# A graph network on one core: self terms moved into an eighth bank between Q and P, thirds and squares given to GpSimd, unread products put ahead of two stages

## What is computed

```python
h = relu(layernorm(x)); x = x + L0(h)                    # two hyperbolic passes inside L0
h = relu(layernorm(x))
src = [edge_src, all nodes]; dst = [edge_dst, all nodes] # a self edge for every node
m = relu(concat(h[src], h[dst]) @ W1 + b1)               # 128 wide
out = segment_sum(m @ W2 + b2, dst) / counts             # counts include the self edge
x = x + out
```

## Time and profile before

| | |
|---|---|
| median of 3 runs | 1189.39 us (1187.72 to 1190.02) |
| the profiled execution: own time, and its span | 1186.87 us, 1185.0 us |
| busy: PE, PEld, DVE, ACT, POOL | 1028.0, 951.0, 1054.7, 712.7, 368.7 us |
| seam 1, from the first fold to the first product of the second pass | 488.75 to 527.21 us |
| seam 2, from the first sum to the spread of group 1 | 636.44 to 700.26 us |
| the edge loop from there | 484.7 us |

### The profile page before, as it was taken

The page is one execution under the profiler, slowest core; times in us unless marked ns, Lnnn a source line. Parts: engine busy times, 40 slices in busy tenths (PEclk is TensorE's granted clock), DMA queues, the critical chain, the costliest instruction groups (busy, mean ns, idle before and its releaser), DMA issues.

```text
span 1185.0 us, 53692 instructions
## 1 busy us (share of the span) xinstructions
PE 1028.0 (87%) x21722; PEld 951.0 (80%) x21722; DVE 1054.7 (89%) x1448; ACT 712.7 (60%) x1933; POOL 368.7 (31%) x268
## 2 busy tenths in 40 slices
PE   3079898989898998728998599999999999999998
PEld 2058777777787877727998479999999999999997
DVE  8879999999999999785664889999999999999995
ACT  5348888888888888520002576665556555666663
POOL 7000000000000000010000037777777777777774
PEclk9569999999999999759999689999999999999999
DMA  2002323232323232579950255444544445444450
GB/s 82 0 33 100 122 95 126 95 126 95 126 95 126 95 122 99 228 284 337 411 244 18 86 172 164 162 160 152 157 156 159 158 159 161 161 161 161 161 161 29
DMA packets 44877, 169.98 MB, mean 143 GB/s; under 512 B 19440, under 2 KB 19766, under 8 KB 44827
## 3 DMA queue, kind: packets, MB, share of 16 engines
q1 hardware_dynamic: 44827, 169.28, 39.7%
HBM read 121.11 MB, written 48.14 MB: 143 GB/s over the span
## 4 chain that ended last, share of the span: by engine, by line
PE 51%; DVE 32%; issue 9%; DVEq 4%; ACT 2%; DMA 1%; SPq 0%; POOL 0%; ACTq 0%; POOLq 0%
PE PS L1563 17%; PE PS L1565 11%; PE PS L1578 8%; PE PS L1436 8%; DVE arena L1055 7%; DVE arena L1032 5%; DVE arena L1040 4%; DVE arena L1018 3%; PE PS L1583 3%; DVE arena L1027 2%; DVEq L361 2%; PE PS L1467 1%; DMA Cw<-slot_rows 1%; DVE arena L1047 1%; DVE aggTw L1066 1%
## 5 line engine op out<-in xcount | busy, mean ns | idle before, releaser
L595 POOL TENSOR_TENSOR arena<-arena 128x512 bf16<-128x512 f32 x240 | 342.3, 1443 | 319.6 <-ACT arena L773 319.6
L1563 PE MATMUL PS<-arena 125*128 125x128 bf16 x3600 | 344.6, 219 | 2.5 <-DVE HTw L1268 1.0
L773 ACT ACTIVATE arena<-arena 128x512 bf16<-128x512 f32 x240 | 150.8, 628 | 187.1 <-DVE arena L1285 187.1
L1563 PEld LDWEIGHTS PS<-arena 125*128 125x128 bf16 x3600 | 250.4, 97 | 9.3 <-issue 5.1
L1436 PE MATMUL PS<-arena,A 125*64 125x72 f32 x4800 | 179.3, 230 | 65.0 <-DVE aggTw L1066 38.4
L1436 PEld LDWEIGHTS PS<-arena,A 125*64 125x64 f32 x4800 | 165.4, 139 | 74.3 <-issue 49.5
L653 ACT ACTIVATE arena<-arena 128x72 bf16<-128x72 bf16 x864 | 216.9, 344 | 1.7 <-DVE arena L1040 1.7
L1285 DVE SCALAR_TENSOR_TENSOR arena<-PS,arena 128x512 f32<-128x512 f32 x240 | 159.4, 679 | 28.7 <-ACT arena L780 28.7
L780 ACT ACTIVATE arena<-PS 128x512 bf16<-128x512 f32 (+2 forms) x336 | 171.9, 547 | 0.0
L1565 PE MATMUL PS<-arena 108*128 108x128 bf16 x1200 | 167.4, 221 | 0.0
L1565 PE MATMUL PS<-arena,HTw 108*128 108x128 bf16 x1200 | 165.8, 219 | 0.0
(11 more groups left out here) (195 smaller groups left out, 1388.5 us busy)
## 6 DMA issues: line engine op xcount, KB each, us to landing
adjacency<-arena SPq DMA_DIRECT2D x48, 900.0 KB, 3.6
arena<-adjacency SPq DMA_DIRECT2D x46, 900.0 KB, 8.0
Bw<-slot_rows SPq DMA_DIRECT2D x48, 800.0 KB, 4.2
Cw<-slot_rows SPq DMA_DIRECT2D x48, 700.0 KB, 4.5
arena<-q_table SPq DMA_DIRECT2D x144, 18.0 KB
q_table<-arena SPq DMA_DIRECT2D x6, 336.0 KB
slot_rows<-slot_row SPq DMA_DIRECT2D x49, 13.0 KB
x_sb<-in_x SPq DMA_DIRECT2D x1, 700.0 KB
```

The source lines that it names most:

```text
L595: nc.gpsimd.tensor_tensor(H3[k][:, at_b, 2, :], Hs[k][:, 4 * q:4 * q + 4, :], H3[k][:, at_b, 1, :], ALU.subtract).then_inc(s_low_set, 1)
L773: nc.scalar.activation(H3[k][:, at_b, 1, :], Hs[k][:, 4 * q:4 * q + 4, :], ACT.Copy).then_inc(s_mid_set, 1)
L1563: mm(ps, OTs[k][:, b, :], P3[:, b, part, :], start=(part == 0), stop=False)
```

## The change

What it does, by place in the program:

- **Self terms** (`self_sum_ps(c)` is the first columns of bank 7): PE makes each quad's self term in bank 7, one bank for all seven, between the Q products: Q0, Q1, S0, Q2, S1, ... Q6, S5, P0, S6, P1 to P6. Each waits until the relu of the one before has emptied the bank (`self_set`). DVE takes the relu instead of ACT, in the iteration of its Q loop that is two quads later.
- **Thirds**: all thirds of Q, and those of the first `PLOWS` = 3 quads of P, are GpSimd's. `spread(0)` waits for the thirds of P quad by quad instead of for all.
- **Squares of seam 1**: GpSimd makes the first `POOLED` = 4, DVE the last 3. The two memsets become eight of at most `CLEAR` = 800 columns, `aggTw` first, before `rows_ps` is waited for.
- **Unread products**: `keep_warm` issues 50 bf16 products of 128x128 by 128 columns, whose result is not read, before the second pass (released by `due` in the middle of `linear(1)`) and before the transposes (released by `due` behind the first sums of the layer norm).
- The first load to `Cw` is released when the layer norm's squares are summed (`squares_summed`). The addition of the bias b2 moves behind the one-hot matrices of group 0's sums.

```diff
@@ -40,6 +40,10 @@
 OWN = 4096.0
+PLOWS = 3
+WARM = 50
+POOLED = 4
+CLEAR = 800
 WHOLE = 12582912.0
...
@@ -459,7 +470,7 @@
                 load_sources(0)
-                sp.wait_ge(norm_in, 2 * len(PIECES))
+                sp.wait_ge(squares_summed, 1)
                 load_destinations(0)
...
@@ -575,12 +586,19 @@
                 if l == 1:
+                    for c in range(POOLED):
+                        pool.wait_ge(fold_set, c + 1)
+                        pool.tensor_tensor(quad_of(square_words, c), quad_of(aggTw[0:F, :], c),
+                                           quad_of(aggTw[0:F, :], c), ALU.mult).then_inc(sq_first, 1)
                     with pool.If(fast == 1):
                         pool.wait_ge(ht_set, len(QUADS))
-                        pool.wait_ge(sq_set, len(QUADS))
-                        pool.wait_ge(rows_ps, 1)
-                        pool.memset(degree, 0.0).then_inc(agg_cleared, 1)
-                        pool.memset(aggTw[:, :], 0.0).then_inc(agg_cleared, 1)
+                        pool.wait_ge(sq_first, POOLED)
+                        pool.wait_ge(sq_rest, len(QUADS) - POOLED)
+                        for table in (aggTw, degree):
+                            if table is degree:
+                                pool.wait_ge(rows_ps, 1)
+                            for a in range(0, NW, CLEAR):
+                                pool.memset(table[:, a:min(a + CLEAR, NW)], 0.0).then_inc(agg_cleared, 1)
                 with pool.If(fast == 0):
...
@@ -600,7 +618,18 @@
+            def quad(table, c):
+                return table[:, QUADS[c][0]:QUADS[c][-1] + 1]
             with pool.If(fast == 1):
+                for c in range(len(QUADS)):
+                    pool.wait_ge(q_second, c + 1)
+                    pool.tensor_tensor(quad(Q3, c)[:, :, 2, :], quad(RQ, c), quad(Q3, c)[:, :, 1, :],
+                                       ALU.subtract).then_inc(q3_set, 1)
+                for c in range(PLOWS):
+                    pool.wait_ge(p_second, c + 1)
+                    pool.tensor_tensor(quad(P3, c)[:, :, 2, :], quad(RP, c), quad(P3, c)[:, :, 1, :],
+                                       ALU.subtract).then_inc(p3_first, 1)
                 turns(pool, low_parts)
...
@@ -761,12 +790,6 @@
-            for c, bs in enumerate(QUADS):
-                sc.wait_ge(self_ps, c + 1)
-                nc.scalar.activation(RT[:, 0:N].rearrange("f (p b) -> f b p", b=NB)[:, bs[0]:bs[-1] + 1, :],
-                                     bank(c)[:, 0:PN * len(bs)].rearrange("f (b p) -> f b p", p=PN),
-                                     ACT.Relu).then_inc(self_set, 1)
             def middle(g, k, q):
...
@@ -854,10 +876,12 @@
-            def layer_norm(dst, source):
+            def layer_norm(dst, source, second=False):
...
                     link(ve.tensor_reduce(row(T1)[:, b], source[:, b, :], X, ALU.add))
+                if second:
+                    ve.sem_inc(due, 1)
                 for b in PIECES:
...
@@ -865,6 +889,8 @@
                     link(ve.tensor_reduce(row(T2)[:, b], C[:, b, :], X, ALU.add))
+                if second:
+                    ve.sem_inc(squares_summed, 1)
                 ask(ve.tensor_scalar(a_, row(T2), 1.0 / F, 1e-5, ALU.mult, ALU.add))
...
@@ -919,6 +945,8 @@
                 ts(row(ATN), row(T3), ARTANH[0], ALU.mult)
+                if l == 1:
+                    ve.sem_inc(due, 1)
                 for c in ARTANH[1:]:
...
@@ -1197,10 +1225,10 @@
                                          quad_of(aggTw[F:2 * F, :], c), ALU.add).then_inc(fold_set, 1)
-                    for c in range(len(QUADS)):
+                    for c in range(POOLED, len(QUADS)):
                         ve.wait_ge(fold_set, c + 1)
                         ve.tensor_tensor(quad_of(square_words, c), quad_of(aggTw[0:F, :], c),
-                                         quad_of(aggTw[0:F, :], c), ALU.mult).then_inc(sq_set, 1)
+                                         quad_of(aggTw[0:F, :], c), ALU.mult).then_inc(sq_rest, 1)
                     ve.wait_ge(rows_ps, 1)
...
@@ -1245,17 +1273,26 @@
             tt(x_sb[:, :, :], x_sb[:, :, :], A[:, :, :], ALU.add)
-            layer_norm(A[:, :, :], x_sb[:, :, :])
+            layer_norm(A[:, :, :], x_sb[:, :, :], True)
...
             ts(row(Z), row(Z), 1.0, ALU.add, 1.0, ALU.max)
+            ve.sem_inc(counts_read, 1)
             link(ve.reciprocal(row(Z), row(Z)))
-            tt(x_sb[:, :, :], x_sb[:, :, :], b2b[P_, :].unsqueeze(1).broadcast_to([PN, NB, F]), ALU.add)
             link(ve.memset(RT[:, N:NW], 0.0))
...
                 return table[:, QUADS[c][0]:QUADS[c][-1] + 1]
+            def add_bias():
+                ve.tensor_tensor(x_sb[:, :, :], x_sb[:, :, :], b2b[P_, :].unsqueeze(1).broadcast_to([PN, NB, F]),
+                                 ALU.add).then_inc(bias_set, 1)
+            def self_relu(c):
+                ve.wait_ge(self_ps, c + 1)
+                ve.tensor_scalar(quad_of(RT, c), self_sum_ps(c).rearrange("f (b p) -> f b p", p=PN), 0.0, None,
+                                 ALU.max).then_inc(self_set, 1)
...
@@ -1295,21 +1332,25 @@
                             .then_inc(q_read, 1)
-                    if c:
-                        ve.wait_ge(q_second, c)
-                        ve.tensor_tensor(quad(Q3, c - 1)[:, :, 2, :], quad(RQ, c - 1), quad(Q3, c - 1)[:, :, 1, :],
-                                         ALU.subtract).then_inc(q3_set, 1)
+                    if c > 1:
+                        self_relu(c - 2)
                 for c in range(len(QUADS) + 1):
...
                             .then_inc(p_rest, 1)
-                    if c:
+                    if c == 0:
+                        self_relu(len(QUADS) - 1)
+                    if c > PLOWS:
                         ve.wait_ge(p_second, c)
...
                                          ALU.subtract).then_inc(p3_set, 1)
-                ve.wait_ge(p3_set, len(QUADS))
-                ve.wait_ge(q3_set, len(QUADS))
+                ve.wait_ge(p3_first, PLOWS)
+            with ve.If(fast == 0):
+                add_bias()
+                for c in range(len(QUADS)):
+                    self_relu(c)
+                ve.wait_ge(self_set, len(QUADS))
             with ve.If(fast == 0):
...
@@ -1340,13 +1381,14 @@
                 sum_onehots(0, 0)
-                ve.wait_ge(self_ps, len(QUADS))
+                add_bias()
                 turns(ve, add_step)
...
                 any_order(2)
+            ve.wait_ge(bias_set, 1)
             ve.sem_inc(fin_ps, 1)
...
@@ -1360,6 +1402,11 @@
             halves = (slice(0, F), slice(F, HID))
+            def keep_warm(at):
+                for _ in range(WARM):
+                    mm(bank(at)[:, 256:384], identb[:, :], onesb[:, :], start=True, stop=True)
...
@@ -1497,6 +1544,8 @@
                 else:
+                    pe.wait_ge(due, 1)
+                    keep_warm(6)
                     with pe.If(fast == 1):
...
@@ -1524,27 +1576,43 @@
             last.then_inc(counts_ps, 1)
+            pe.wait_ge(due, 2)
+            keep_warm(0)
             transposes(1)
-            for c, bs in enumerate(QUADS):
+            def q_product(c):
                 pe.wait_ge(ht_quad, len(QUADS) + c + 1)
-                for i, b in enumerate(bs):
+                for i, b in enumerate(QUADS[c]):
                     for ps in node_halves:
...
                 last.then_inc(q_ps, 1)
-            for c, bs in enumerate(QUADS):
+            def p_product(c):
                 pe.wait_ge(q_read, c + 1)
-                for i, b in enumerate(bs):
+                for i, b in enumerate(QUADS[c]):
                     for ps in node_halves:
...
-            for c, bs in enumerate(QUADS):
-                pe.wait_ge(p_rest, c + 1)
-                o = bank(c)[:, 0:PN * len(bs)]
+            def self_term(c):
+                if c == 0:
+                    pe.wait_ge(counts_read, 1)
+                else:
+                    pe.wait_ge(self_set, c)
+                bs = QUADS[c]
                 for half in halves:
-                    last = mm(o[half, :], W1ab[:, half], HT[:, bs[0]:bs[-1] + 1, :].rearrange("f b p -> f (b p)"),
-                              start=True, stop=True)
+                    last = mm(self_sum_ps(c)[half, :], W1ab[:, half],
+                              HT[:, bs[0]:bs[-1] + 1, :].rearrange("f b p -> f (b p)"), start=True, stop=True)
                 last.then_inc(self_ps, 1)
+            q_product(0)
+            for c in range(1, len(QUADS)):
+                q_product(c)
+                self_term(c - 1)
+            p_product(0)
+            self_term(len(QUADS) - 1)
+            for c in range(1, len(QUADS)):
+                p_product(c)
...
@@ -1552,7 +1620,10 @@
                     if not from_second(g):
-                        pe.wait_ge(self_set, q + 1)
+                        if q < PLOWS:
+                            pe.wait_ge(p3_first, q + 1)
```

(4 more changed lines are left out.)

16 lines of the change are left out of this document (11 added, 5 removed).

## The result

The changed kernel takes 1209.48 us (median of 5 runs, 1208.44 to 1210.94) against 1188.67 us for the kernel before (1187.72 to 1190.02, 5 runs): a ratio of 1.0179, 95% interval 1.0165 to 1.0192. It is slower by 1.8%. The forecast was 1206.5 us.

The account below looks back on a forecast made before the run. Bound: the last third of Q, delayed by a new loop in the Q stage. Seam 2 +17.3 and seam 1 0 gave 1204.2 on the profiled 1186.87, 1206.7 on the runs' median; forecast 1206.5 us, 8-in-10 range 1196 to 1216.

Parts of the forecast that it names:

- The loop: Q stage, seam 2: one quad in flight through PE, ACT and DVE; a round 4.66 us at full clock, 6.5 at half.
- The fall of the clock: Q stage: PE at half speed from about 677 us, since it works 1.9 of 4.66 us a round.
- The term of +16.1: Seam 2: last third of Q at 697.4 instead of 681.3 us.
- Transposes and one-hots: Seam 2: transposes take 2.7 instead of 5.42 us; one-hot matrices end at 670.6 instead of 673.5.
- Rival C: Clock not granted in the unread products or lost behind them; transposes and first Qs at half: +22 to +27, 1214; chance 0.13.
- if the clock comes back some 6 us into P's unbroken products: P stage, seam 2: last third of P at 709.5, DVE free at 712.7: +17.3 us.
- the other branch, +21.2: P stage, seam 2: clock does not come back in P's products; DVE free at 716.6 us.
- Seam 1: Between the passes: stall -1.3, clock -0.2, folds held by GpSimd's squares +1.5; sum 0 us.
- A granted clock for the first block: Second pass, first product block: 3.62 us would halve, but DVE's second piece gates it; gain at most some 0.5, put at -0.2.
- Rival B: Same Q rounds but PE keeps full clock: +9.0 to +11.3, 1198 to 1201 us; chance 0.12.
- D: Rounds overlap, Q stays at ACT's 1.2 us per quad, last third 1.5 us earlier: 1186 us; chance 0.06.
- rival A: The forecast itself: Q rounds one behind another, mostly at half clock; 1201 to 1213 us; chance 0.66.

Follow-up runs that it names:

- the first two experiments: Against changed kernel: self terms back behind P in P's banks, relus on ScalarE, 1187.00 us; VectorE's relu of self term c-2 ahead of quad c's rest, 1197.66 us.
- self terms late: Changed kernel with self terms put back behind P, in P's banks, relus on ScalarE: 1187.00 us, ratio 0.9999.
- filled rounds: Changed kernel with 36 unread products of 128 columns ahead of each of four self terms: 1203.40 us, ratio 1.0142.

## Why the prediction was right, and where it was off

- **The loop.** Right in place and mechanism: the order of VectorE and one bank make it, and the first two experiments show it, since the relu put first takes 10.7 us away and the self terms put late all of it. Its round at half clock was 6.04, not 6.5: the handovers between engines take 0.02 to 0.04 us each where 0.07 to 0.2 were allowed, the relu 0.98 on the chain (1.05 by itself) for 1.1, Q 1.73 for 1.9, the self term 1.93 for 1.8. At full clock 4.37 (with the filler) for 4.66.
- **The fall of the clock.** Expected about 677, came at about 675, one round earlier. The first round at half clock and the shorter others cancel: from LN end to the last third of Q it is 31.0 us where the forecast had 31.2. The term of +16.1 measured +15.9.
- **Transposes and one-hots.** Forecast 2.7 us and 4.4 us behind LN end; measured 2.86 and 4.5. Rival C, the unread products too short or their clock lost in the pause behind them, did not come about in this profile. That was in part luck: the same block lost its clock ahead of the transposes in six of the eleven profiles that have it, two of them (self terms late, filled rounds) with nothing changed ahead of that point.
- **The step that failed: "if the clock comes back some 6 us into P's unbroken products, as it did behind 665.41".** It did not. P ran for 8.75 us on the chain at 0.50 with TensorE fully busy, and so the other branch, +21.2, was the better one. Why it stayed there is open. LN end to spread(1) measured +20.1 against the +17.3 that went into the sum. The range allowed for it.
- **Seam 1.** Stall -1.3 forecast, -1.4 measured and the whole clearing put back brings 2.00 again. The folds were mis-sized: +1.5 forecast, +3.0 measured, since a strided square takes 1.98 us on GpSimd beside a fold (7.90 for four; none ran alone), between the plain row's 1.44 and the 2.5 of the upper bound, and each of four folds came as long after the one before it, 1.9 to 2.0 us. The Trainium skill (SBUF — State Buffer, Who interferes with whom) says that a VectorE instruction with two SBUF inputs contends with one of GpSimd that reads SBUF; the folds beside the squares agree. A granted clock for the first block was put at -0.2; it gains nothing there, and the next block takes 1.0 us more than in the run without unread products (1.84 to 3.38 us in the ten other profiles with them). Sum 0 forecast, +1.7 measured.
- **The total.** +17.3 in the forecast. Measured +20.1 in seam 2 and +1.7 in seam 1; the rest (-2.1, +1.3, +0.2, +0.2) comes out near nothing. The second pass by itself took from 107.1 to 112.0 us over the profiles of this study, so that its +1.3 isn't explained and is no part of the change that could be shown. Rival B (the clock stays) and D (no loop) are out by the profile. Two bounds of the forecast don't follow from their own terms: a last third at 691.0 is 9.7 us behind 681.3 and not 9.0, and rival A's terms give some 1203 to 1214, not 1201 to 1213. Neither decides anything here.

## What to carry to other kernels

An extra bank helps only with what can overlap in it: if one bank is written by one engine, read by a second, and the second's queue holds the reading behind work that waits for the first engine's next product, it is a loop with one item in flight, and its length is a sum over all engines. Write that round down from both queues before costing anything by throughput, and look first at which of two independent instructions stands first on the reader: that alone was 10.7 us here. And a pause that a new order puts into TensorE's work is not priced by its length: here 1.17 us of waiting stood ahead of some 24 us at the half clock.

## What the runs showed of the hardware

- Being busy did not bring the clock back. With self terms between the P products TensorE worked 2.00 of 2 us in every stretch from 678 to 700 us and stayed at 0.50; in the changed kernel it did so for 9 us of P's products. Within the spread's bf16 products it came back each time, 3 to 5 us behind their start (711.15 to about 716, 696.90 to about 701, 697.16 to about 700). That the slow products were f32 isn't enough to tell them: the f32 transposes of 125 rows in the kernel before regained the clock in some 6 us behind 665.41, the last half of a microsecond with Q products. What sets the products of 64 and 65 rows apart wasn't tried. They hold the clock where they find it: with the self terms late the same products ran at 1.00 from 670 to 686. The Trainium skill (TensorE: Matmul & The Clock Gate, part 1) says that sustained activity lifts the half rate; by busy time these two stretches do not bear it out.
- A VectorE operation could last until one of GpSimd beside it had ended: an operation of 0.18 us (L860) took 0.70 beside clearings of 0.7 us, and 2.00 beside one of 2.76; folds came 1.9 to 2.0 us apart beside squares of 1.98 us, and 1.1 to 1.2 without (7.29 us for 6.25). It isn't so for every operation: in the kernel before, the next one took its 0.19 us beside the second clearing.

```profile
507.10 2.80 POOL L583 MEMSET aggTw<- 128x3197 f32 x1
507.23 0.19 DVE L835 TENSOR_TENSOR rows<-rows 125x25 f32<-125x25 f32 x1
```

- VectorE's relu of 128x500 from PSUM to elements that lie 25 apart took 1.05 to 1.14 us, against 0.69 for the dense subtraction of 125x512.
